# A two-phase block kernel: the second phase one step further behind the first, silu(z) evicted in the next step, x read transposed

## The reference

```
xz = x @ W_in                     # 256 -> 1024; halves x_proj and z, 512 channels each
x_conv = silu(causal conv of x_proj, 4 taps, per channel)
ssm = x_conv @ W_xproj            # 512 -> 33: delta, B (16), C (16)
h_mean = sum over tokens of x_conv x (softplus(delta) * B) / 2048   # per sequence, 512 x 16
y = (C @ h_mean + D * x_conv) * silu(z)
x1 = layernorm(x + y @ W_out)
q = fp4 quantise and dequantise, in blocks of 16
h = silu(q(x1) @ q(w_gate)^T) * (q(x1) @ q(w_up)^T)                 # 256 -> 704
out = layernorm(x1 + q(h) @ q(w_down)^T)
```

## Time and profile before

| | |
|---|---|
| median of 3 runs (lowest, highest) | 2201.66 us (2200.06 to 2202.36) |
| profiled execution, its own time | 2204.03 us |
| its span, first to last instruction | 2202.1 us |
| mean granted TensorE clock | 0.98 of full speed |
| busy: PE / DVE / ACT / POOL | 90% / 80% / 50% / 51% |
| DMA, mean use of its engines | 12.2% |

### The profile page before, as it was taken

The page is one execution under the profiler, slowest core; times in us unless marked ns, Lnnn a source line. Parts: engine busy times, 40 slices in busy tenths (PEclk is TensorE's granted clock), DMA queues, the critical chain, the costliest instruction groups (busy, mean ns, idle before and its releaser), DMA issues.

```text
span 2202.1 us, 37847 instructions
## 1 busy us (share of the span) xinstructions
PE 1990.6 (90%) x10532; PEld 1583.8 (72%) x10532; DVE 1756.7 (80%) x3548; ACT 1111.5 (50%) x2100; POOL 1115.6 (51%) x1643
## 2 busy tenths in 40 slices
PE   1887899899999999899999999899999999877776
PEld 1655688688877888688877888688876888666665
DVE  6234788798978888789877888798887888788875
ACT  2665455555545555455544556455544555423332
POOL 2223455466545556455644555465554556445543
PEclk9999999999999999999999999999999999999998
DMA  2111111111111111111111111111111111000000
GB/s 79 50 56 43 34 49 44 44 43 45 49 41 34 44 48 45 36 49 49 41 38 41 44 44 48 38 49 44 39 41 39 49 45 35 29 20 25 20 20 15
DMA packets 77089, 90.53 MB, mean 41 GB/s; under 512 B 8881, under 2 KB 59953, under 8 KB 76849
## 3 DMA queue, kind: packets, MB, share of 16 engines
q1 hardware_dynamic: 76848, 87.73, 12.2%
HBM read 37.37 MB, written 16.78 MB: 25 GB/s over the span
## 4 chain that ended last, share of the span: by engine, by line
PE 76%; issue 5%; DVE 4%; ACT 3%; POOL 1%; ACTq 0%; DVEq 0%; POOLq 0%
PE pgu L489 23%; PE pd L489 14%; PE pd L537 9%; PE pa L489 6%; PE pb L489 6%; PE pc L571 4%; PE pc L519 4%; PE pe_ L631 2%; PE pa L559 2%; PE pc L496 2%; PE pe_ L548 1%; PE pd L638 1%; DVE hbuf L990 1%; DVE qsh L820 1%; PE pa L615 1%
## 5 line engine op out<-in xcount | busy, mean ns | idle before, releaser
L489 PE MATMUL pgu<-wgu_hi,xqT 128*128 128x512 f32 (+1 forms) x1536 | 427.7, 387 | 0.9 <-issue 0.9
L489 PE MATMUL pd<-wd_hi,hqT 128*128 128x256 f32 (+1 forms) x1536 | 334.5, 299 | 18.7 <-DVE r L1012 15.5
L489 PEld LDWEIGHTS pgu<-wgu_hi,xqT 128*128 128x128 f32 x1536 | 279.8, 190 | 75.8 <-issue 27.6
L537 PE MATMUL pd<-wout,g 128*128 128x256 f32 x1024 | 259.9, 398 | 49.6 <-DVE hqT L980 35.2
L489 PEld LDWEIGHTS pd<-wd_hi,hqT 128*128 128x128 f32 (+1 forms) x1536 | 255.8, 190 | 57.4 <-issue 23.8
L946 DVE SCALAR_TENSOR_TENSOR acc<-xps,cw,acc 128x512 f32<-128x512 f32 x256 | 248.7, 972 | 24.4 <-POOL acc L429 23.7
L418 POOL TENSOR_SCALAR rs<-mv 128x1 f32<-128x1 f32 x128 | 61.6, 481 | 396.4 <-DVE mv L1027 228.8
L537 PEld LDWEIGHTS pd<-wout,g 128*128 128x128 f32 x1024 | 191.5, 195 | 79.7 <-issue 56.0
L741 ACT ACTIVATE hqT<-pe_ 128x512 fp32r<-128x512 f32 x128 | 76.2, 595 | 335.3 <-PE pe_ L631 335.3
L402 POOL TENSOR_TENSOR xv<-xnq,qsx 128x256 f32<-128x256 bf16 x128 | 79.5, 621 | 300.1 <-DVE xnq L839 300.1
L489 PE MATMUL pgu<-wgu_lo,xqT 128*128 128x512 f32 (+1 forms) x768 | 228.3, 379 | 0.0
(11 more groups left out here) (132 smaller groups left out, 4669.2 us busy)
## 6 DMA issues: line engine op xcount, KB each, us to landing
xcr<-xcs SPq DMA_DIRECT2D x128, 256.0 KB, 2.3
xin<-in_L_attn_x_dram SPq DMA_DIRECT2D x32, 512.0 KB, 3.9
xres<-in_L_attn_x_dram SPq DMA_DIRECT2D x128, 128.0 KB, 2.1
out_dram<-outb SPq DMA_DIRECT2D x128, 128.0 KB, 1.7
szr<-in_L_attn_W_in_dram SPq DMA_DIRECT2D x1, 1024.0 KB, 7.4
szr<-in_L_ffn_w_down_dram SPq DMA_DIRECT2D x1, 704.0 KB, 8.6
szr<-in_L_ffn_w_gate_dram SPq DMA_DIRECT2D x1, 640.0 KB, 4.5
szr<-in_L_ffn_w_up_dram SPq DMA_DIRECT2D x1, 640.0 KB, 5.7
```

Of the source, the lines that this page charges most:

```text
L489: mm = pe.matmul(bank, lhsT, rhs, start=(m == 0), stop=(m == len(pairs) - 1))
L537: mm = pe.matmul(pd[:, 0:DM], g[:, (s + 1) % 2, c, j * P:(j + 1) * P], wout[:, c, :], start=(c == 0), stop=(c == NB - 1))
```

## The change

1. x comes from the host a second time as `x_t`, transposed (features on partitions). `xin` becomes 128 x 2 x 512, loaded by SP at j = 0 after `xt_h` and `xt_l` of the supertile before. PE's eight transposes go. ACT's `split_x` and DVE's `rest_of_x`, one instruction of 1024 columns each, read `xin` at the end of step j = 3 for the next supertile; the first one stands ahead of the walk.
2. y runs one step later: `y_product`, `y_skip` and `gate` of step w work on channel block w - 1 (17 steps behind phase one). At s = 0, j = 0 that is the last block of the old sequence, whose state is at hand. At s = 0, j = 1 (`mid_y`) they stand mid-step. `late_y` is gone, gate and up stand in their own step. The output projection stays at w - 4.
3. `silu_z` of channel block v = u - 1 is called in step u, ahead of the silu of the gate product (at s = 0, j = 1 after the first tap). `z_product` of step u still waits for all earlier blocks' eviction. `silu_z` waits for `g_ready` >= w, the gate that stands in this same step.
4. ACT and DVE, like SP, loop one sequence less.

```diff
-            def silu_z(i, j, s, u, w):
-                act.wait_ge(z_pe, u + 1)
-                if exists(i, NSUP):
-                    act.wait_ge(g_ready, w + 1)
-                act.activation(szr[:, j, s, :], pb[:, :], ACT.Silu).then_inc(z_ready, 1)
+            def silu_z(j, s, v, w):
+                jz, sz = ring_place(s, j)
+                act.wait_ge(z_pe, v + 1)
+                at_least(act, g_ready, w)
+                act.activation(szr[:, jz, sz, :], pb[:, :], ACT.Silu).then_inc(z_ready, 1)
+
+            def split_x(sg):
+                act.wait_ge(xin_landed, 16 * (sg + 1))
+                at_least(act, z_pe, 4 * sg)
+                act.activation(xt_hi[:, :, :], xin[:, :, :], ACT.Copy).then_inc(xt_h, 1)
...
+                    if exists(v) and not mid_y:
+                        silu_z(j, s, v, w)
                     if exists(tg):
                         act.wait_ge(gu_pe, tg + 1)
...
-                    if not late_y(j, s) and p1:
-                        silu_z(i, j, s, u, w)
...
+                    if j == 3 and exists(sg + 1, NSUP):
+                        split_x(sg + 1)
-            walk(body, act.Fori)
+            split_x(0)
+            walk(body, act.Fori, last=2)
...
+            def rest_of_x(sg):
+
+                dve.wait_ge(xt_h, sg + 1)
+                dve.tensor_tensor(xt_lo[:, :, :], xin[:, :, :], xt_hi[:, :, :], ALU.subtract).then_inc(xt_l, 1)
...
-                    p1, p2 = exists(sg, NSUP), exists(i, NSUP)
+                    p1, p2 = exists(sg, NSUP), exists(w - 1)
...
-                    if j == 0 and p1:
-
-
-                        pe.wait_ge(xin_landed, 16 * (sg + 1))
-                        at_least(pe, xct_copied, v)
-                        at_least(pe, z_ready, u)
-                        for k in range(KM):
-                            for t in range(TPS):
-                                mm = pe.transpose((pa, pb)[k][:, t * P:(t + 1) * P],
-                                                  xin[:, t, k * P:(k + 1) * P], ident[:, :])
-                            mm.then_inc(xt_pe, 1)
-
-                    after_late = j == 1 and late_y(0, s)
-                    if p2 and not late_y(j, s) and not after_late:
-                        y_product(j, s, b, i, w, capped(v, NT))
-                    if exists(tg) and not after_late:
+                    mid_y = j == 1 and seq_start(s)
+
+                    if p2 and not mid_y:
+                        y_product(i, j, s, b, w - 1, capped(v, NT))
+                    if exists(tg):
                         gate_and_up(tg)
...
-                    if not late_y(j, s) and p1:
+                    if p1 and not mid_y:
                         z_product(j, s, u, sg)
+                    if mid_y and p2:
+                        y_product(i, j, s, b, w - 1, capped(v, NT))
```

126 lines of the change are left out of this document (65 added, 61 removed).

## The result

| | before | after |
|---|---|---|
| median (lowest, highest) | 2201.91 us (2200.06 to 2202.36), 4 runs | 2376.44 us (2367.32 to 2393.04), 4 runs |
| ratio, 95% interval | | 1.0799 (1.0746 to 1.0851) |
| profiled execution, its span | 2202.1 us | 2372.5 us |
| mean granted TensorE clock | 0.980 | 0.957 |

The change costs 175 us where 61 were forecast, and the time lies above the stated range (2195 to 2335). The direction, and the wait of z's product for its bank, are as forecast; two terms, the one on x and the one on the start of a sequence, had the wrong sign.

The account below looks back on a forecast made before the run. PE, busy 90% of the span, was taken as the bound. Terms -20.4 - 2 - 10.5 - 36 - 5 + 104 + 10 + 21 = +61 us on 2204.0 gave 2265, as a median 2263 us; range 2195 to 2335.

Parts of the forecast that it names:

- The wait that the change adds: z's product waits for its silu, which waits for the gate, at j = 3, 0, 1: +104 us, plus +10 in first supertiles.
- the 0.3 for all that isn't z's own wait: Per ordinary supertile, later ACT instructions and a late ssm product add 0.3 us to z's 4.87.
- x off PE: Dropping PE's eight transposes of x gains 20.4 us in ordinary supertiles, 2 in filling ones, 10.5 in phase one.
- ACT and DVE carry no more than before: split_x and rest_of_x do the elements of the two instruction pairs they replace, so they add no load.
- second rival: The loop binds but POOL's part is shorter, 0.6 us less in each of 66 waits: 2202 us, chance 0.12.
- any work taken off PE is gained in full: In ordinary supertiles PE hardly stops, so the transposes' 1.02 us would be gained whole in each of 20.
- The fourth rival: One small term misfires, for instance halves of x late for j = 0: 2294 us, chance 0.04.
- In phase one -10.5: In four supertiles of phase one alone, transposes and PE's wait for the halves, 2.6 us each, go: -10.5 us.
- The start of a sequence: From state product to y of j = 2, 19.6 us become 13.6: -36 us over six, -5 for the last sequence.
- it starts when it started before: At a sequence's j = 0 the state product, waiting about 2.5 us for dB instead of 1.08, starts no later: no gain.
- The clock, +21: One in four or five of 66 new waits is followed by a slow clock costing 1.42 us: +21, bounds 0 and 94.
- The third rival: The clock falls at nearly every wait: 2336 us, chance 0.13.

Follow-up runs that it names:

- the run with the silu first: The phases alone plus POOL's second norm behind the gate, with ACT's silu of z ahead of its two copies of h: 2263.90 us, ratio 1.0268.
- The phases alone: The changed kernel without its part on x, so PE transposes x as before: 2334.44 us, ratio 1.0603.
- The two runs that open the loop: Changed kernel with POOL's second norm behind the gate: 2281.35 us; changed kernel with the gate multiplying by a constant tile, silu of z not waiting: 2293.27 us.
- x alone: The kernel before with only the part on x (transposed from the host, split at the end of j = 3): 2263.21 us, ratio 1.0278.
- the subtraction early: x alone, with ACT's high-half copy ahead of its wait for POOL's nm and DVE's subtraction ahead of the second residual: 2201.78 us, ratio 0.9991.
- the residual: The phases alone plus second norm behind the gate, with DVE taking the output projection's residual ahead of y_skip at s = 0, j = 1: 2257.79 us, ratio 1.0236.

## Why the prediction was right and wrong

- **"The wait that the change adds", +104: the mechanism is right, the size was too small.** In the changed kernel the three waits are 1.55, 1.95 and 1.57, 5.07 us for 4.87, and an ordinary supertile is 65.6 us without a slow clock, where the sum gives 60.0 - 1.02 + 5.17 = 64.15. The term should have been 6.6 per supertile, 132 us. What was mis-sized is the 0.3 for all that isn't z's own wait: it is 1.5 to 1.6, in gaps too small for a bracket and in what the brackets leave out (0.4 in every step of 13.6, which the run with the silu first takes back). The phases alone say the same: by the prediction's own working they wait 1.74, 0.37 (1.39 - 1.02, as they keep the transposes) and 1.74; measured are 1.53, 0.32 and 1.57, and supertiles of 64.9 against 60.0, 4.9 where 4.15 would follow. The two runs that open the loop confirm its parts, among them that the norm ahead of the gate binds. At j = 0 of the changed kernel the 1.39 became 1.95, as the subtraction makes the gate late.
- **"x off PE", -33: the sign was wrong, measured +60.** Two steps failed. "ACT and DVE carry no more than before" counted elements and not operands: the source moved from PSUM to SBUF, and 2 x 0.69 us became 2.19 in the place where it stands. The rule was on the page that the prediction itself cites for its second rival, the Trainium skill, SBUF — State Buffer, "Who interferes with whom": a VectorE instruction with two SBUF inputs contends with a GpSimd one that reads SBUF. The trace agrees (1.18 us for four columns beside POOL's 1.39). It was applied to what was there and not to the new instruction. And "any work taken off PE is gained in full" looked at PE's rows alone: a row without a bracket says that PE doesn't wait, not by how much the others are ahead. The dequantised h was 1.49 us ahead at j = 0 and 0.22 in x alone; with the subtraction early 0.3 of the 1.02 us per supertile arrived, and PE waits 0.67 for that h. The fourth rival had this part go wrong, but by PE waiting for the halves of x; in ordinary steps PE did not wait for them, and it was DVE's next instructions, and with them the silu of the convolution, that came late.
- **In phase one -10.5: wrong.** The halves of x were to be ready ahead of their reader. But `split_x` stands at the end of ACT's list for j = 3, behind the copy of the transposed convolution (79.55), and where there is no gate and up product in between nothing covers it: `pa` waits 2.89 us for the low half, against 1.57 before. In x alone the fourth state product starts at 183.5 us, where it was 183.0, so the time of the transposes was just given back. That z's product in phase one would wait for a silu behind softplus and its table (2.33 us) was not seen. Together the first four supertiles grew by 12.0 us.
- **"The start of a sequence", -36 and -5: did not arrive.** From the state product to y of j = 2 it was 23.55 us and is 21.62: -1.9, not -6.0. The waits of 1.49 and 0.42 us and the clock of 0.62 behind them are most of the rest. And "it starts when it started before" was wrong: from gate and up of j = 0 to the state product it was 16.53 (1142.32 to 1158.85) and is 19.72 (1241.05 to 1260.77), as z's product and its wait of 1.74, counted as none, now stand in it; the wait for `dB` of 2.68 was forecast as 2.5. Net +1.3 in place of -6.0, six times: 44 us. Behind the last state product, where -5 was forecast, -0.7 is left. Of the signs that the prediction named, z's waits, ACT's waits for the gate and the missing 2.4 us ahead of the output projection are there; the shorter first supertile of a sequence is not.
- **The clock, +21: too small, up to 58.** In the phases alone it is (122 - 91) / 2 = 16 us, as forecast; in x alone (165 - 91) / 2 = 37 of its 60. The large share comes from j = 0, where waits were not foreseen. The third rival (it falls at nearly every wait) is not what is seen: at the same wait of 1.94 to 1.95 us it fell in some supertiles and not in others.

Sum: x is off by 93 us (60 for -33). The phases alone are off by 59: with the transposes kept the working gives -36 - 5 + 104 - 20 + 10 + 21 = 74, and 133 were measured. The two together were forecast 20 above the sum of the parts (the wait at j = 0 takes back what the transposes give) and came out 18 below it: 93 + 59 - 38 = 114, which is 175 - 61. What is settled by runs is the two parts, the loop, and the place of copy and subtraction. What a start of a sequence would need in order to gain was tried in one piece (the residual) and is open, and so is what is left of the 1.02 us when nothing collides.

## What to carry to other kernels

Before work is taken off the bounding engine, read how far ahead the others are: at the next instruction that waits for them, the gap between their end and its start, not the absence of a wait (here 1.49 us, of which 0.22 were left, so that a delay of 1.05 us on POOL reached PE). When an operand moves from PSUM to SBUF, price the instruction anew and look at what GpSimd does at that moment; a few lines' difference in the place of one 1.2 us instruction was worth 61 us. A wait put between two engines that already follow each other closes a loop: measure it around, and shorten it by moving out what it does not need (three tiny instructions, 95 us).

## What the hardware showed that was not expected

- A DVE subtraction of 128 x 4 elements from two SBUF tiles took 1.18 us and ended with POOL's multiplication (the shortest of its line took 0.16); full size (128 x 1024) took 1.22 us clear of it and 2.19 beside it. POOL was held up too: its 0.22 us instruction took 1.07 when it started behind DVE's subtraction, and its 0.46 took 1.51 although its row starts 0.25 us ahead of it (571.64 and 571.89).
- More work on PE did not make the kernel slower: with 365 useless products, 84 us of work, it took 2365 us for 2376, and the clock stayed up in all ordinary steps of that trace. Without them, waits of 1.94 to 1.95 us at j = 0 were followed by half clock in eight supertiles of twenty and by full clock in the others.
- No kernel beat the one before. The best, x alone with the subtraction early, ties with it (0.9991, 0.9973 to 1.0009).
